# The maxima's transposes written to unused columns of an S bank, and every word of the order dealt out anew

## What is computed

```python
x = x + tanh(g_xattn[0]) * xattn(layernorm(x), ctx)      # 16 heads of depth 16
x = x + tanh(g_ffn[0]) * ffn(layernorm(x))

def xattn(q, kv):
    qh, kh, vh = heads(q @ wq + bq), heads(kv @ wk + bk), heads(kv @ wv + bv)
    attn = softmax(einsum('bhqd,bhkd->bhqk', qh, kh) / 4)
    return einsum('bhqk,bhkd->bhqd', attn, vh) @ wo + bo

def ffn(x):                                              # top 2 of 8 from a router
    p = top_k(softmax(x @ router_w), 2); p = p / sum(p)
    return (gelu(x @ w1 + b1) @ w2 + b2) * sum(p)
```

## Time and profile before

| | us |
|---|---|
| median of 3 runs | 709.57 (709.5 to 710.0) |
| span of the profiled execution, first to last instruction | 1105.9 |
| PE busy in it | 1088.8 (98%) |
| DVE, ACT, POOL busy in it | 526.6, 408.3, 329.7 |
| mean granted TensorE clock in it | 0.556 |

### The profile page before, as it was taken

How to read it: one execution, slowest core, us unless ns; L and a number is a source line. 1 busy time by engine, 2 the same in 40 slices (tenths; PEclk the granted TensorE clock), 3 DMA queues, 4 the chain that set the end, 5 groups by cost and what they waited for, 6 DMA issues and landing times.

```text
span 1105.9 us, 20672 instructions
## 1 busy us (share of the span) xinstructions
PE 1088.8 (98%) x7648; PEld 972.5 (88%) x7648; DVE 526.6 (48%) x1299; ACT 408.3 (37%) x797; POOL 329.7 (30%) x474
## 2 busy tenths in 40 slices
PE   5999999999999999999999999999999999999998
...
PEclk7555555555555555555555555555555555555555
...
GB/s 189 187 124 140 78 99 31 74 69 74 99 52 71 52 74 99 52 95 28 74 98 52 117 14 83 82 64 110 42 61 70 74 99 52 63 24 10 2 10 17
DMA packets 47797, 80.27 MB, mean 73 GB/s; under 512 B 10997, under 2 KB 30802, under 8 KB 47698
## 3 DMA queue, kind: packets, MB, share of 16 engines
...
...
## 4 chain that ended last, share of the span: by engine, by line
PE 97%; SPq 1%; DVE 1%; DMA 0%; POOL 0%; issue 0%; ACT 0%; POOLq 0%
PE P L951 48%; PE S L980 13%; PE OT L1010 12%; PE T L992 12%; PE P L1036 4%; PE TR L1019 2%; PE TR L1095 2%; PE TR L1026 1%; PE TR L1078 1%; PE TR L1063 1%; SPq L430 1%; PE TR L966 1%; DMA CTRAW<-in_ctxT 0%; DVE NEGM L783 0%; POOL CT_LO L591 0%
## 5 line engine op out<-in xcount | busy, mean ns | idle before, releaser
L783 DVE TENSOR_REDUCE NEGM<-S 112x1 f32<-112x375 f32 x512 | 272.3, 542 | 186.5 <-PE S L980 181.9
L703 ACT ACTIVATE PROBS<-T 125x448 f32<-125x448 f32 x384 | 204.2, 543 | 208.1 <-PE T L992 199.7
L980 PE MATMUL S<-KS,QS 96*112 96x376 f32 x512 | 239.6, 484 | 1.7 <-DVE NEGM L783 1.7
L992 PE MATMUL T<-QS,KS 98*125 98x224 f32 x768 | 209.1, 376 | 0.0
L992 PEld LDWEIGHTS T<-QS,KS 98*125 98x125 f32 x768 | 169.6, 244 | 22.9 <-issue 7.1
L1010 PE MATMUL OT<-PROBS,VA 125*17 125x112 f32 x3072 | 140.1, 364 | 0.0
L980 PEld LDWEIGHTS S<-KS,QS 96*112 96x112 f32 x512 | 118.3, 239 | 19.1 <-issue 10.2
L1010 PEld LDWEIGHTS OT<-PROBS,VA 125*17 125x17 f32 x3072 | 107.4, 128 | 21.0 <-issue 9.3
L606 POOL CAST HT_HI<-HG 128x224 fp32r<-128x224 f32 x124 | 45.9, 370 | 256.5 <-ACT HG L729 255.1
L729 ACT ACTIVATE HG<-P,B 128x224 f32<-128x224 f32 x128 | 57.3, 447 | 123.2 <-PE P L951 123.2
L951 PE MATMUL P<-W_HI,HT_LO 128*112 128x256 f32 x256 | 98.9, 386 | 0.0
(11 more groups left out here) (112 smaller groups left out, 1817.5 us busy)
## 6 DMA issues: line engine op xcount, KB each, us to landing
...
KS<-KLO SPq DMA_DIRECT2D x128, 94.0 KB, 2.7
...
```

Of the source, the lines that this page charges most:

```text
L703: act.activation(PT[0:KN, k, pp * 4 * SQ:(pp + 1) * 4 * SQ], T_BANK[i % 2][0:KN, 0:4 * SQ], ACT.Exp, scale=SCALE).then_inc(exp_done, 1)
L783: dve.tensor_reduce(NEGM[:, b.par, col:col + 1], S_BANK[i % 2][0:SQ, 0:SK], AX.X, ALU.max, negate=True).then_inc(max_done, 1)
L980: pe.matmul(S_BANK[i % 2][0:SQ, 0:SKP], QS[0:96, b.gpar, i % 2, i // 2, b.j * SQ:(b.j + 1) * SQ], KS[0:96, b.ring, i // 2, :], start=True, ...
L992: mm = pe.matmul(T_BANK[i % 2][0:KN, r * 2 * SQ:(r + 1) * 2 * SQ], KS[0:98, prv.ring, pair, k * KN:(k + 1) * KN], QS[0:98, prv.gpar, :, pa ...
```

## The change

PE's transpose of the maxima no longer writes to TR but to 112 columns of S bank 1 behind the scores, which use 376 of 512. It no longer takes part in the turns of TR. Instead the S word 1 of a batch waits for MLO of the batch before, besides the maxima, and mt waits for the previous MLO.

```diff
+        MT = S_BANK[1][0:NH, SKP + 8:SKP + 8 + SQ]
...
-                        act.activation(MHI[:, :], TR[0:NH, 0:SQ], ACT.Copy).then_inc(mhi_done, 1)
+                        act.activation(MHI[:, :], MT, ACT.Copy).then_inc(mhi_done, 1)
...
-                        dve.tensor_tensor(MLO[:, :], TR[0:NH, 0:SQ], MHI[:, :].bitcast(F32),
+                        dve.tensor_tensor(MLO[:, :], MT, MHI[:, :].bitcast(F32),
...
                     if op == "mt" and prv.exists:
-                        take("TR", mlo_done, prv.count(1, 1))
+                        if past(prv.count(1)):
+                            pe.wait_ge(mlo_done, prv.count(1))
                         pe.wait_ge(max_done, prv.count(16, 16))
-                        pe.transpose(TR[0:NH, 0:SQ], NEGM[:, prv.par, :], IDENT[0:SQ, 0:SQ]).then_inc(mt_ready, 1)
+                        pe.transpose(MT, NEGM[:, prv.par, :], IDENT[0:SQ, 0:SQ]).then_inc(mt_ready, 1)
                     if op == "s" and b.exists:
...
+                        if i == 1 and past(b.count(1)):
+                            pe.wait_ge(mlo_done, b.count(1))
```

The lists are all new. Their number of words is the same; many lists of `SPECIAL` are down to one word, since their words now stand in a neighbour's list with another offset. Two lines of the even step's list:

```diff
-    """st.5+1 dh.0+2 s.11+1 n2+1 dn.0+2 st.6+1 wo+1 x2n+2 st.7+1 s.12+1 st.8+1 dh.1+2 st.9+1 dn.1+2 kd.0+1
+    """st.4+1 ql+1 cl+1 s.10+1 st.5+1 dh.0+2 n2+1 s.11+1 dn.0+2 rt s.12+1 st.6+1 st.7+1 s.13+1 wo+1 x2n+2 lo.0
```

More of the change, by code:

```diff
@@ new lines @@
+    """st.4+1 ql+1 cl+1 s.10+1 st.5+1 dh.0+2 n2+1 s.11+1 dn.0+2 rt s.12+1 st.6+1 st.7+1 s.13+1 wo+1 x2n+2 lo.0
+       kd.1+1 st.8+1 rx s.14+1 kd.0+1 s.15+1 k.0 dh.1+2 st.9+1 lo.1 lo.2 dn.1+2 k.1 st.10+1 x2t mt s.0 st.11+1
+       pv.0+1 pv.1+1 pv.2+1 pv.3+1 lo.3 kd.0 s.1 up.0 s.2 xn up.1 s.3 up.2 s.4 ol+1 rw.0 up.3 s.5 s.6 up.4 rw.1
+       au+1 up.5 s.7 lo.4 up.6 s.8 rw.2 ct s.9 lo.5 up.7 s.10 n1 m st.0 s.11 ct-1 st.1 s.12 v.2+1 s.13 xt st.2
+       rw.3 s.14 st.3 v.0 s.15 v.1 st.4 rw.4 xb+1 q.0 st.5 v.2 mt-1 n2 s.0-1 kd.1 st.6 xl q.1 st.7 rw.5 s.1-1
+       st.8 k.0-1 st.9 s.2-1 lo.6 k.1-1 st.10 s.3-1 st.11 s.4-1 pv.0 rw.6 pv.1 pv.2 lo.7 pv.3 l1-2 s.5-1 st.0-1
+       s.6-1 rw.7 st.1-1 v.0-1 m-1 v.1-1 s.7-1 au qs st.2-1 s.8-1 st.3-1 wo n1-1 s.9-1""",
```

69 lines of the change are left out of this document (36 added, 33 removed).

## The result

| | before | after |
|---|---|---|
| median, same chip | 709.79 us (709.50 to 711.58, 4 runs) | 733.45 us (729.94 to 737.08, 4 runs) |
| ratio | | 1.0286, 95% interval 1.0234 to 1.0337 |
| profiled execution | 1105.9 us at clock 0.556 | 731.3 us at clock 0.995 |

The changed kernel is 2.9% slower. The forecast was 712.6, 3.0 us above the kernel before, with a range up to 719: the side was right, the size was not (the loss is 23.7 us), and the time lies outside the range.

The account below looks back on a forecast made before the run. It took the profiled execution to be bound by PE's own columns. For the median, 709.57 + 0.3 (start) + 3.0 (steady pairs) = 712.9, stated as 712.6; range 704 to 719, the forecast's own 711 to 715.

Parts of the forecast that it names:

- the ruler: Up stage: one S matmul to the next, 1.34 us in the profile, was put at 0.745 us at full clock.
- The bank: Maxima's transposes moved to S bank 1: new wait for MLO covered, 0, bounds -0.2 to +0.3 us per pair.
- The start: Reordered first loads: PE begins at 10.5, first S at 31.2; net +0.3 us, bounds -1.3 and +3.
- The steady pair: Repeated pair of batches: three narrower places cost 0.1 to 1.0 us; taken as +0.2 a pair, +3.0 in all.
- The first narrow place: Up stage, s.5 and s.6 without an up between: a wait of 0.3 us, 0.1 with words 10% longer.
- The other two: In the pair, s.9 to s.13: wait 0 to 0.3 us; q.0 taking v.0's bank: 0 to 0.4 us.
- The discount: Steady pair: low part of 0.1 to 1.0 us taken, since hidden fixed costs make words longer than estimated.
- Tail: End of the kernel: words kept from the last AU on but for one up; 0, bounds -1 and +1.
- Weights' chain: Six links of load, ACT cast and POOL subtraction, with less PE work beside them: 0, bound +2.
- The third, "clearly slower": Three narrow places cost 0.8 us a pair and the start 2: 720 at most, 718 likely; chance 0.13.
- The first: Rival: faster, as PE's waits at the pair's end go; 704 to 708, most likely 705.5; chance 0.35.
- The fourth: Rival: moved transposes wait for the S bank as long as for TR; reorder alone, within the forecast; no separate chance.

Follow-up runs that it names:

- e1: The changed code (maxima's transpose in the S bank, S word 1 waiting for MLO) with the word order of the kernel before: 731.90 us, ratio 1.0277.
- before's second profile: The unchanged kernel profiled once more, for a profile at the clock of the timed runs: span 712.9 us.
- e3: The changed kernel with one context load (cl) moved on SP from behind the q stores to ahead of m: 727.22 us, ratio 1.0219.
- e4: e3 with the word xn moved from the up stage to just behind x2t: 724.49 us.
- e6: e3 with both xn moved behind x2t and k.1 moved behind st.10: 718.81 us, ratio 1.0106.
- e11: e6 with the router weights' word rw.5 (WN) moved from behind st.7 to behind v.2: 716.96 us, ratio 1.0050.
- e5: e3 with k.1, the second half of K, moved behind st.10: 726.42 us.
- e2: The kernel before with the new word order only, transposes of the maxima in TR as before: 785.09 us, ratio 1.1031.

## Why the prediction was wrong, point by point

- **What bounds the kernel: half right.** PE does, but the ruler was 10% short. PE's times at the low clock, scaled by 0.556, gave 0.745 us from an S word to the next and 37.6 a pair; at full clock these are 0.84 and 41.56. What I called 105 us "that are not columns" is mostly PE too: busy 685.8 of 712.9 us.
- **The bank (0, bounds -0.2 to +0.3 a pair): right for this order.** PE's wait of S words for MLO comes to 0.6 us in the whole of after. The bound was for a cover that thins; where it goes (e1), the price is 1.1. The chain of 1.3 us that the prediction read in the earlier trace rows was right: e1 has 1.36.
- **The start (+0.3): right in the sum, by errors that cancel.** The first matmul was put at 10.5 and came at 9.88, the first xt at 14.6 and 14.81, and no gap of 3 us stands before the second. But the first S came at 33.97, not 31.2 (28.84 in before's second profile), and still the first transpose is at 48.2 in both. The clock, by the windows of before and of after, was indeed higher with the gaps gone, and fell later:

```profile
12.00:24.00 12.00, 6.12 (x35) 0.75 0.78 223
24.00:36.00 12.00, 5.60 (x30) 0.78 0.51 138
36.00:50.00 14.00, 12.69 (x70) 0.91 0.65 187
```

```profile
12.00:24.00 12.00, 9.56 (x39) 1.00 0.51 155
24.00:36.00 12.00, 7.70 (x47) 0.97 0.79 206
36.00:50.00 14.00, 12.82 (x61) 0.78 0.64 166
```

  (Columns: window, length, PE busy and its matmuls, clock, DMA share, GB/s.) This does not repeat: with the same start lists the first of these windows has 0.72 to 0.77 in e3, e4, e6 and e11, and 1.00 in e5. By the rule of the Trainium skill ("TensorE: Matmul & The Clock Gate", section "HAM oscillation — how this bites in real kernels") the start would have given -1.0. The trace of after agrees in that the clock of the first window, in which PE stands still less, is higher, 1.00 instead of 0.75, but not that it pays: it gave nothing by the first transpose.
- **The steady pair (+0.2 a pair, +3.0 in all): the step that failed.** It measured +1.36, 13.6 us in ten pairs. The first narrow place was real, 0.38 us against the 0.3 worked out and 0.1 kept, since XN took 1.22 us (1.21 in after) and not the 0.73 of the earlier trace rows. The other two (s.9 to s.13, q.0 behind v.0) show no wait in e3's pair. Missing from the sum were two things: the context load that the lists moved behind six stores on SP (e3: 0.6 us of the 1.36) and k.1's bank behind KLO (some 0.2 to 0.4: e5's best pair is 0.2 shorter than e3's, and the two rows around the wait lose 0.40). What makes the last 0.18 stays open. I had checked each S word's bank and never the SP queue past the start, nor what POOL does beside VectorE.
- **The discount.** I took the low end of 0.1 to 1.0 because "words are longer than my ruler". They were, but VectorE's waits are not a matter of PE's length when they start at a DMA.
- **Tail (0, bounds -1 and +1):** -1.6.
- **Weights' chain (0, bound +2):** +5.5 ahead of the 9th transpose, but at other places. From 50 to 200 us PE is busy for 144.7 us in after and for 148.9 in before, and most of the difference is two stops for a P bank whose KLO came late, of 1.29 and 1.21 us. The first:

```profile
87.45 0.57 ACT L685 ACTIVATE KHI<-P,BK 128x376 fp32r<-128x376 f32 x1 [2.31 <-DMA KS<-KHI]
88.72 0.44 PE L957 MATMUL P<-CT_HI,WK_HI 128*128 128x376 f32 x1 [1.29 <-DVE KLO L797]
```

  ACT's KHI stands there until SP's move of the last KHI has landed (2.31 us, at the second stop 2.65). Ahead of the first stop, that move (issued from 82.36 on) stands on SP behind the moves of KLO; before, it goes ahead of them (76.47), and no such stop of PE is in the profile. So this too looks like a DMA's place on SP. No run tried it by itself, and with the same start lists PE is busy for 147.8 us in e6, so the amount is not settled.
- **Rivals.** The third, "clearly slower", was the right one in kind and too low: it held only bank waits. Its sum, 709.6 + 12 + 2, is also 723.6 and not the 720 that stands there, so the range up to 719 left out part of the rival's own case. The first fell with the second profile of before, where PE has next to no wait at a pair's end either. The fourth fell with the profile of after, where the moved transposes wait for another engine 0.2 us in all, and with e2, since without the edit the new lists cost 10%.
